# A fused attention and FFN layer on one core: no fp32 copies of keys and queries in DRAM, each x chunk loaded once, the last two query chunks in the key buffers

## The reference, cut to what matters

```python
# x: (1, 4096, 256) fp32, 16 heads of 16
ct_q  = x @ Wd_q + b                        # 256 -> 128
query = heads(ct_q @ Wu_q + b) + heads(rope(ct_q @ Wq_r + b))
ct_kv = x @ Wd_kv + b                       # 256 -> 128
key   = heads(ct_kv @ Wu_k + b) + heads(rope(x @ Wk_r + b))
value = heads(ct_kv @ Wu_v + b)
attn  = softmax(query @ key.T / scale)      # per head, 4096 x 4096
x = layernorm(x + (attn @ value) @ Wo + bo)
x = layernorm(x + int8_ffn(x))              # one scale from max|x| of all rows
```

## Time and profile before

| what | value |
|---|---|
| median of 3 runs | 1960.79 us |
| the profiled execution's own time | 1961.84 us |
| its span | 1960.0 us |
| PE busy | 1864.4 us (95%) |
| ACT busy | 1801.4 us (92%) |
| DVE busy | 1574.0 us (80%) |
| POOL busy | 160.0 us (8%) |
| first exponential of attention starts at | 152.11 us |

### The profile page before, as it was taken

How to read it: one execution, slowest core, us unless ns; L and a number is a source line. 1 busy time by engine, 2 the same in 40 slices (tenths; PEclk the granted TensorE clock), 3 DMA queues, 4 the chain that set the end, 5 groups by cost and what they waited for, 6 DMA issues and landing times.

```text
span 1960.0 us, 31470 instructions
## 1 busy us (share of the span) xinstructions
PE 1864.4 (95%) x12996; PEld 455.1 (23%) x12996; DVE 1574.0 (80%) x1499; ACT 1801.4 (92%) x2022; POOL 160.0 (8%) x132
## 2 busy tenths in 40 slices
PE   8779999999999999999999999999999999999975
PEld 3342122122222222222222222222222122222234
DVE  4644988888888888888888888888988898888477
ACT  3239999999999999999999999999999999999955
POOL 6541800000000000000000000000000200000011
PEclk9889999999999999999999999999999999999987
DMA  5755111101111111111111111111121011111002
GB/s 166 239 178 195 25 25 25 25 20 19 21 17 25 25 25 25 25 25 26 25 28 59 17 16 26 25 25 25 25 47 25 17 18 18 24 26 25 1 24 86
DMA packets 166966, 84.15 MB, mean 43 GB/s; under 512 B 130304, under 2 KB 146944, under 8 KB 166336
## 3 DMA queue, kind: packets, MB, share of 16 engines
q1 hardware_dynamic: 162784, 75.51, 16.2%
q10 hardware_dynamic: 4032, 6.56, 1.1%
HBM read 51.48 MB, written 29.23 MB: 41 GB/s over the span
## 4 chain that ended last, share of the span: by engine, by line
ACT 61%; PE 21%; issue 10%; DVE 4%; DMA 2%; POOL 1%; SPq 0%; ACTq 0%; DVEq 0%; POOLq 0%
ACT arena L856 60%; PE PS L660 10%; PE PS L611 7%; PE PS L1141 2%; PE PS L699 1%; PE PS L1113 1%; DVE arena L916 1%; PE PS L1272 1%; DMA arena<-arena 1%; DMA arena<-xT_dram 1%; DVE bn L787 1%; DVE parts_or_sums L1528 0%; DMA k_whole<-arena 0%; POOL arena L1423 0%; POOL arena L1422 0%
## 5 line engine op out<-in xcount | busy, mean ns | idle before, releaser
L856 ACT ACTIVATE arena<-PS 128x1024 f32<-128x1024 f32 x1860 | 1708.1, 1336 | 18.5 <-PE PS L611 18.3
L660 PE MATMUL PS<-arena,Vh 128*32 128x512 f32 x8192 | 1094.6, 607 | 6.0 <-DVE arena L916 4.0
L611 PE MATMUL PS<-Qst,Kst 49*128 49x512 f16 x4096 | 727.9, 384 | 23.5 <-ACT arena L856 2.8
L916 DVE SCALAR_TENSOR_TENSOR arena<-arena 128x2048 f32<-128x2048 f32 x282 | 645.8, 2290 | 0.1
L892 DVE TENSOR_SCALAR arena<-PS 128x512 int32<-128x512 f32 x376 | 259.4, 690 | 254.4 <-PE PS L611 251.1
L611 PEld LDWEIGHTS PS<-Qst,Kst 49*128 49x128 f16 x4096 | 190.3, 93 | 1045.7 <-ACT arena L856 1018.0
L660 PEld LDWEIGHTS PS<-arena,Vh 128*32 128x32 f32 x8192 | 161.5, 108 | 314.8 <-issue 299.1
L912 DVE SCALAR_TENSOR_TENSOR arena<-arena 128x2048 f32<-128x2048 f32 x94 | 216.4, 2302 | 0.0
L900 DVE TENSOR_SCALAR arena<-arena 128x2048 int32<-128x2048 int32 x94 | 115.6, 1230 | 7.7 <-DVE arena L916 0.5
L902 DVE TENSOR_SCALAR arena<-arena 128x2048 int32<-128x2048 int32 x94 | 116.8, 1242 | 0.0
L1141 PE MATMUL PS<-arena,w 128*128 128x512 f32 x176 | 86.8, 638 | 21.9 <-DMA arena<-xT_dram 15.6
(11 more groups left out here) (118 smaller groups left out, 483.4 us busy)
## 6 DMA issues: line engine op xcount, KB each, us to landing
Kst<-k_halves SPq DMA_DIRECT2D x64, 128.0 KB
Qst<-q_halves SPq DMA_DIRECT2D x64, 128.0 KB
Vh<-head_values SPq DMA_DIRECT2D x30, 256.0 KB, 5.5
arena<-xT_dram ACTq DMA_DIRECT2D x10, 512.0 KB, 4.8
k_halves<-parts_or_sums SPq DMA_DIRECT2D x16, 256.0 KB, 2.9
k_whole<-arena SPq DMA_DIRECT2D x8, 512.0 KB, 3.8
q_halves<-parts_or_sums SPq DMA_DIRECT2D x16, 256.0 KB, 2.7
q_whole<-arena SPq DMA_DIRECT2D x8, 512.0 KB, 4.0
```

Source lines behind the costliest of these rows:

```text
L611: return nc.tensor.matmul(out, Kst[par][low:low + HK + 1, at:at + 128], Qst[par][low:low + HK + 1, j * CH:(j + 1) * CH], start=True, stop= ...
L660: last = nc.tensor.matmul(bank(value_bank(t))[32 * j:32 * j + 32, :], Vh[t % 2][:, kt, :], moving, start=kt == first, stop=kt == last_kt)
L856: nc.scalar.activation(ring(at, k), bank(g % SLOTS * SLOT, k), ACT.Exp, scale=EXP_SCALE).then_inc(a.exp, 1)
L916: last = nc.vector.scalar_tensor_tensor(out=t, in0=t, scalar=POLY[3 - j], in1=power if j == 3 else mantissa, op0=ALU.add, op1=ALU.mult)
```

## The change

**Stores.** The fp32 wholes `k_whole` and `q_whole` and their 16 stores of 512 KB are gone, and with them ACT's waits for them. The general path loads weights, x and tables and projects keys and queries again when it runs.

**x.** `DQ_` of chunks 4 to 7 stands behind the key chain's `KR_` and `DKV` instead of ahead of `QR_`, so each x chunk is loaded once (eight loads instead of twelve). All four latents of these chunks are held, in four `ctq` places.

**Buffers.** q6 and q7 use the key buffers (`SLOT_OF`), so none of q4 to q7 waits for another of them.

**Later places.** The key lengths of chunks 4 to 7 are taken just before `QHI` of chunk 7, the key maximum's transposes before value products 1 and 4, the first shift behind value product 5. The second query lengths stand behind the first three score groups of attention, and the second shift behind all value products. ACT then waits for DVE's last step before it loads the table of the exponential. SP stores the first shift right behind q4's halves, which is ahead of the tables of q7.

```diff
     for c in late:
-        order += [("p", c, KR_)] + [("p", c + 1, DKV)] * (c + 1 < NCH) + [("p", c, UK_), ("p", c, KHI)]
-    order.append(("p", HALF_CH, DQ_))
+        order += [("p", c, KR_)] + [("p", c + 1, DKV)] * (c + 1 < NCH) + [("p", c, DQ_), ("p", c, UK_), ("p", c, KHI)]
     for c in late:
-        order += [("p", c + 1, DQ_)] * (c + 1 < NCH) + [("p", c, QR_), ("p", c, UQ_), ("p", c, QHI)]
+        order += [("p", c, QR_), ("p", c, UQ_), ("p", c, QHI)]
...
+def make_slots():
+
+    slots, passed = {}, {}
+    for c, n in PARTS:
+        slot = ("k" if c >= NCH - 2 else n), c % 2
+        before = passed.setdefault(slot, [])
+        slots[c, n] = slot, len(before), (before[-1] if before else None)
+        before.append((c, n))
+    return slots
+
+
+SLOT_OF = make_slots()
+SLOT_PARTS = {slot: sum(of == slot for of, _, _ in SLOT_OF.values()) for slot, _, _ in SLOT_OF.values()}
...
-        ctq = [cut(12 * K1 + p * CH, (CH,)) for p in range(2)]
+        ctq = [cut((12, 21)[p // 2] * K1 + p % 2 * CH, (CH,)) for p in range(4)]
...
+            behind_first()
...
-                    sp.dma_start(chunk_of(dst), parts[n][c % 2][:, part, :, :]).then_inc(s_parts[n][c % 2], 16)
-
-            def store_whole(c, n):
-                half, at = divmod(c, HALF_CH)
-                dst = k32_dram[:, c * CH:(c + 1) * CH] if n == "k" else q32_dram[half, :, at * CH:(at + 1) * CH]
-                sp.dma_start(chunk_of(dst), C[n][c % 2]).then_inc(s_whole[n][c % 2], 16)
+                    sp.dma_start(chunk_of(dst), parts[m][p][:, part, :, :]).then_inc(s_parts[m][p], 16)
...
@@ -1000,11 +1015,9 @@
                 next_tables(c, (c, "q"))
                 for n in "kq":
                     store_parts(c, n)
-                    store_whole(c, n)
             for c in range(HALF_CH, NCH):
                 next_tables(c, (c, "k"))
                 store_parts(c, "k")
-                store_whole(c, "k")
...
                 next_tables(c + HALF_CH, (c, "q"))
                 store_parts(c, "q")
-                store_whole(c, "q")
+                if c == HALF_CH:
+                    store_shift(0)
                 if c == HALF_CH + 1:
-                    store_shift(0)
...
-                if p == ("p", HALF_CH + 3, DQ_):
+                if p == ("p", HALF_CH + 3, QHI):
 
                     pe.wait_ge(s_kmax, 1)
                     lengths("k", 1, K_LENGTH_BANK)
-                if p == ("p", HALF_CH + 2, UQ_):
+                if p == ("v", 0, 1):
                     pe.wait_ge(s_ev, in_bank(SMALL_BANK))
                     pe.wait_ge(s_kmax, 3)
                     nc.tensor.transpose(PS[0:1, SMALL_BANK * CH:SMALL_BANK * CH + 128], kmax[:, 2:3], ident[:, :]).then_inc(s_kt, 1)
-                if p == ("p", HALF_CH + 3, QR_):
+                if p == ("v", 0, 4):
                     pe.wait_ge(s_kmax, 5)
                     nc.tensor.matmul(PS[:, SMALL_BANK * CH + 128:SMALL_BANK * CH + 129], kmax_row[0:1, 32:160], ones[0:1, 0:1],
                                      start=True, stop=True).then_inc(s_kt, 1)
-                if p == ("v", 0, 13):
-                    lengths("q", 1, Q_LENGTH_BANKS[1])
...
+            attention_tensor(pe, fast, lambda: lengths("q", 1, Q_LENGTH_BANKS[1]))
...
-                if c >= 2:
+                if before:
                     if e in (KR_, QR_):
-                        act.wait_ge(s_dve, STEP["add", c - 2, n])
+                        act.wait_ge(s_dve, STEP["add", *before])
                     if e in (UK_, UQ_):
-                        act.wait_ge(s_dve, STEP["low", c - 2, n])
-                        act.wait_ge(s_whole[n][par], 16 * (c // 2))
-                    if e == DQ_:
-                        act.wait_ge(s_mm, DONE["p", c - 2, QHI])
+                        act.wait_ge(s_dve, STEP["low", *before])
+                if e == DQ_ and c >= 4:
+                    act.wait_ge(s_mm, DONE["p", c - 4, QHI])
...
-                if p in LAST_OF_X and LAST_OF_X[p] + 2 < len(LOADS):
-                    load_x(act, LAST_OF_X[p] + 2)
-                if p == ("p", HALF_CH + 3, UQ_):
+                if p[0] == "p" and p[2] == KHI and p[1] + 2 < NCH:
+                    load_x(act, p[1] + 2)
+                if p == ("v", 0, 5):
                     shifts(0)
-                if p == ("v", 0, 14):
-                    shifts(1)
-
-            for n in "kq":
-                for par in range(2):
-                    act.wait_ge(s_whole[n][par], 16 * HALF_CH)
+            shifts(1)
+
+            act.wait_ge(s_dve, len(STEP))
             nc.scalar.activation(xs[:, 0:1], small[:, 6:7], ACT.Exp)
```

More of the change, by code:

```diff
@@ L194, with tables_of @@
 ROTATED = {p: 3 * (n + 1) for n, p in enumerate(PARTS)}
-LOADS = list(range(NCH)) + list(range(HALF_CH, NCH))
-def load_of(c, n):
+TABLES = list(range(NCH)) + list(range(HALF_CH, NCH))
+def tables_of(c, n):
     return c if n == "k" or c < HALF_CH else c + HALF_CH
-LAST_OF_X = {("p", c, KHI): c for c in range(NCH)}
-LAST_OF_X.update({("p", c, DQ_): c + HALF_CH for c in range(HALF_CH, NCH)})
+def make_slots():
[8 more added lines that the diff above has]
+SLOT_PARTS = {slot: sum(of == slot for of, _, _ in SLOT_OF.values()) for slot, _, _ in SLOT_OF.values()}
 def make_vector_steps():
@@ L1116, in product @@
                     return
-                load = load_of(c, "q" if e in Q_GROUPS else "k")
-                x2 = [xT[load % 2][:, k, :] for k in range(2)]
-                kv, cq = ctkv[:, c * CH:(c + 1) * CH], ctq[c % 2]
+                x2 = [xT[c % 2][:, k, :] for k in range(2)]
+                kv, cq = ctkv[:, c * CH:(c + 1) * CH], ctq[c % 4]
                 lhsT, rhs = {
@@ L1215, in _, with again @@
             with pe.If(bad == 1):
+                pe.wait_ge(t_w, 16)
+                pe.wait_ge(fast.added, KT // 2)
+                for at, (half, cc, n) in enumerate(AGAIN):
+                    latent, turned_w, up = (W_DKV, W_KR, W_UK) if n == "k" else (W_DQ, W_QR, W_UQ)
+                    x2 = [again_x[:, k, :] for k in range(2)]
+                    def again(b, products):
+                        for k, (lhs, moving) in enumerate(products):
+                            last = nc.tensor.matmul(bank(b), again_w[:, lhs:lhs + 128], moving, start=k == 0, stop=k == len(products) - 1)
+                        return last
+                    pe.wait_ge(t_in, 32 * (at + 1))
+                    if at:
+                        pe.wait_ge(t_ev, 8 * at - 4)
+                    again(0, [(latent + k * DQ, x2[k]) for k in range(2)]).then_inc(t_mm, 1)
+                    pe.wait_ge(t_ev, 8 * at + 1)
+                    turns = [(turned_w + k * D, x2[k]) for k in range(2)] if n == "k" else [(turned_w, again_c)]
+                    again(1, turns).then_inc(t_mm, 1)
+                    again(2, [(up, again_c)]).then_inc(t_mm, 1)
+                    again(3, [(lhs + 128, moving) for lhs, moving in turns] + [(up + 128, again_c)]).then_inc(t_mm, 1)
                 with pe.Fori(0, NT) as t:
@@ L1303, in evacuate @@
                     return
-                par = c % 2
-                k, q = C["k"][par], C["q"][par]
-                dst = {DKV: ctkv[:, c * CH:(c + 1) * CH], DQ_: ctq[par], KR_: A["k"][par], UK_: k[:, 0, :], KHI: k[:, 1, :],
-                       QR_: A["q"][par], UQ_: q[:, 0, :], QHI: q[:, 1, :]}[e]
+                n = "q" if e in Q_GROUPS else "k"
+                (m, par), _, before = SLOT_OF[c, n]
+                whole, turned_part = C[m][par], A[m][par]
+                dst = {DKV: ctkv[:, c * CH:(c + 1) * CH], DQ_: ctq[c % 4], KR_: turned_part, QR_: turned_part,
+                       UK_: whole[:, 0, :], UQ_: whole[:, 0, :], KHI: whole[:, 1, :], QHI: whole[:, 1, :]}[e]
                 at = {DKV: bias[:, B_DKV:B_DKV + 1], DQ_: bias[:, B_DQ:B_DQ + 1], KR_: bias[:, B_KR:B_KR + 1],
@@ L1563, in _ @@
                     key_row()
-                if (name, n) == ("low", "q") and c == HALF_CH:
+                if (name, n) == ("high", "q") and c == HALF_CH:
                     key_column()
```

140 lines of the change are left out of this document (81 added, 59 removed).

## The result

| | before | after |
|---|---|---|
| median of six runs each, us | 1960.42 (1958.65 to 1962.91) | 1951.3 (1949.64 to 1955.62) |
| ratio to before | | 0.9961, 95% interval 0.9951 to 0.9971 |
| the profiled execution's own time, us | 1961.84 | 1949.75 |
| its span, us | 1960.0 | 1947.9 |
| first exponential of attention at, us | 152.11 | 142.16 |

The kernel is faster by 0.39% where I forecast 0.82%. (The quotient of the two medians would give 0.47%, which lies in the same interval.) The direction was right; the time, 1951.3 against 1944.8, is inside the range, near its upper end. The attention stage is what it was the earlier trace rows: busy by window (columns as there), 1724 us from the first exponential on.

The account below looks back on a forecast made before the run. Attention has ACT and PE full, so the gain is how much earlier its first exponential starts: 152.11 to 136.1, 16.0 us, along tables, POOL, DVE and PE's start. From 1961.84 that gives 1945.8, less 1.05 to the median: 1944.8; range 1937 to 1952.

Parts of the forecast that it names:

- They land 4.5 us later (2.9 to 7.4): 112.7: SP's load of q6's tables, issued at 108.2 after the first head's stack, lands 4.5 us later, at 112.7.
- my bound: Tables landing in 7.4 us instead of 4.5 would leave a gain of 11 us.
- the rest, to the first exponential: After q7's DVE steps: query lengths 0.69, slow PE start 5.0, then ACT's second shift and table load; exponential at 136.1.
- The wait for q7's tables: New wait on POOL: q7's tables, behind the first shift's stores on SP, land at 119.8, after q6's rotation ends at 117.3.
- Rival B: DVE and POOL slow each other; all four query parts cost DVE 7.4 us: 7.3 earlier, 1953.5; chance 0.15.
- Rival A: Tables hide and PE's value products set the start of attention: 26 us earlier, 1934.8; chance 0.20.
- Rivals C and D: C: query parts strictly one after another, 1965.4, chance 0.04. D: store waits only change name, 1960.8, chance 0.03.
- the waits for x: PE's waits for x5, x6 and x7 in the key chain: 0.4, about 3 and 3 us, 6.5 instead of 12.1.
- the key products' end: PE finishes the key products of chunk 7 at 95.5.
- k7's halves: DVE's four steps on k7 and the issue of its store are done at 100.5.
- the slow start: PE, idle since 121.0, starts attention at the 1.2 GHz level: 5.0 us instead of 2.6.
- about 4 us that were hidden before: Cost of the later second shift, second query lengths and table load at the start of attention: about 4 us.

Follow-up runs that it names:

- the control: The changed kernel run once more, unaltered, beside other runs: 1952.56 us, ratio 0.9957 to the kernel before.
- the lengths ahead: Changed kernel with the second query lengths ahead of the start of attention again, not behind the first three score groups: 1950.63 us, ratio 0.996.
- the warm start: Changed kernel with twelve fp32 products that nobody reads on PE behind the value products, to keep it busy before attention: 1951.56 us, ratio 0.9954.
- q7's tables ahead: Changed kernel with q7's tables issued ahead of the first shift's stores instead of behind them: 1953.95 us in one execution.
- own places: Changed kernel with q6's and q7's tables loaded early into the second head's stack buffers, right behind k4's halves: 1947.87 us, ratio 0.9946.

## Why the prediction was half right

**The step that failed** is the forecast's "They land 4.5 us later (2.9 to 7.4): 112.7". The landing took 11.3, outside even my bound. I had the price from a view over all twelve loads of the trace before, and none of those stood right behind the stack: there q6's tables were issued at 119.07, 7 us after the stack's last issue. My own sum moved the load right behind it (108.2) and kept the price of the place that it came from. In six executions with the load there (the changed kernel, the control, the kernel before without stores, the lengths ahead, the warm start, q7's tables ahead) it took 10.2 to 11.4 us from issue to POOL's start.

From the forecast's 136.1 to the measured 142.16 it goes like this, each by start times in the forecast and in the rows above:

| step | forecast | measured | adds |
|---|---|---|---|
| q6's tables issued | 108.2 | 109.59 | +1.39 |
| from there to q6's rotation | 4.5 | 11.36 | +6.86 |
| q6's rotation to q7's (I had a wait for q7's tables there) | 7.1 | 3.79 | -3.31 |
| q7's rotation to DVE's first step of q7 | 4.7 | 6.58 | +1.88 |
| q7's steps | 3.4 | 3.57 | +0.17 |
| the rest, to the first exponential | 8.2 | 7.27 | -0.93 |

The sum is 6.06. The wait for q7's tables, which the late q6 swallowed, hid 3.3 of the first miss; that the time still fell inside my range is partly luck. The +1.9 came on top: it is DVE still at q6 beside POOL's rotation and, for 0.4 of it, POOL's copies into `Vh`.

**Rival B** had the right mechanism and not the weight. It is 1.9 us of this kernel, and it becomes the bound as soon as the tables are in time (own places), when q4's and q5's steps stretch and DVE runs without a pause from 113.4 until PE starts. I gave its price to all four parts or to none; it is paid by the parts that run beside a rotation. The 7.4 us itself was misread: in the kernel before, two small steps of the key maximum (120.74 to 122.01 on DVE) stood among q4's four, about 1.2 us of it. The 7.24 of q5 above has nothing in between. **Rival A**, which has tables in time and PE last, fell: even with all tables in time PE was idle 7.59 us before the start. **Rivals C and D** fell too: the kernel is neither slower nor the same.

**Right:** the end of the waits for stores; the waits for x (0, 2.68, 2.06 against 0.4, 3, 3, whose sum of 6.5 should by my own times have been 6.8); the key products' end (96.4 against 95.5); k7's halves (101.32 against 100.5); PE done with the value products at 122.5 against 121.0; the slow start. The bill for the late start, "about 4 us that were hidden before", is 3.9 by the experiment that takes it back (7.27 less 3.33). I had only half of the slow clock, though. The granted clock as PE starts, in the same window view:

```profile
136.00:140.00 4.00, 4.00 (x18) 1.16 (x17) 0.00 (x0) 0.00 (x0) 0.00 (x0) 0.50 0.59 158
```

That is the 1.2 GHz level, as I expected after a wait, but it also followed x6's wait of 2.68 us (eight passes in 5.37 us instead of 3.4), which I had put at full speed. The length of the wait does not settle it: in the kernel before, a wait of 3.04 us was followed by four passes in 1.96, which is full speed. In the control x7's wait was 3.59 and its passes slow too, and k7's rotation began at 96.83 instead of 94.03:

```profile
82.18 5.37 PE L1152 MATMUL PS<-arena,w 128*128 128x512 f32 x8 [3.59 <-DMA arena<-xT_dram]
```

That is most of what made these profiles differ by 1 to 3 us ahead of 100 us (97.39 with the lengths ahead, 97.17 with q7's tables ahead), and why single profiles were compared from q7's last step on.

**What the gain is made of.** I explained the change as one of many parts. By the kernel before without its stores, the deletion of the stores and of ACT's waits for them is all of it (0.9944 against 0.9961 and 0.9957, with intervals that overlap), and perhaps more than all. Without them k7 and q4 move forward, q6's tables come to stand right behind the stack, and q7 ends on DVE at 135.16, against 134.89 with the whole change. The single load of x and the key buffers for q6 and q7 make PE and ACT earlier where nobody waits for them (read from these traces; no run has either of them alone), and the later places exchange 6.59 us behind q7 for 7.27. The best kernel without extra products on PE, 1944.21, has these parts with the tables out of the jam and the lengths back ahead of the start. Whether they add anything there is not shown: no run moves the tables in the kernel that lacks only the stores. Open is what in the stack's eight DMAs takes those 11 us, while the DMA engines were busy 0.36 to 0.57 of the time on average: no run changed their size.

## What to carry to other kernels

Price a DMA by what stands ahead of it in its own ring at the place to which your change moves it, not by the median over places it never had; then a small load that others wait for goes ahead of the bulk, to another ring, or early into memory of its own. When such a wait goes, ask what the engines do to each other once they run without pauses: here DVE beside POOL needed 7.2 us for what it does alone in 3.5. And test the parts of a change one by one: the simplest one gave the whole gain here, and the order behind the last wait (lengths and a table load behind it or ahead of it) was worth another 3.9 us in the profile, and 3.7 between the medians once the tables were in time (1947.87 and 1944.21).

## What the runs showed of the hardware that I had not expected

- A load of 128 KB issued right behind eight DMAs in SP's ring let its reader start after 10.2 to 11.4 us; from ACT's ring at the same moment after 6.1; behind four small stores after 4.4.
- Beside a POOL rotation all four DVE steps stretch, the fp16 copy too, which has one input: 0.69 to 1.67 or 1.75, 0.69 to 1.57, 0.69 to 1.64, 1.22 to 2.29 us; POOL's instructions go from 1.25 to as much as 2.24 (at 46.73 in the changed kernel). The maximum over PSUM stayed at 0.69 in every row, also beside a rotation (106.69 in the changed kernel). This agrees with the Trainium skill, "SBUF — State Buffer", section "Who interferes with whom": it lists casts among the operations that can take the shared port for their whole length and says that a reduction on this chip never does.
- After 2 to 4 us of idle PE's next eight fp32 passes took 5.37 us in most executions and 3.67 in others (after waits of 2.07 and 2.06, and of 2.60 and 2.59, each pair in two kernels that are alike up to there), so two executions can differ by 1.7 us from this alone.
